# Sorting the tokens of two stages by expert, in a fused attention and mixture-of-experts block

## The chip, the cores and the metric

The kernel runs on one core of one Trainium2 chip, with its own five engines: TensorE (PE), VectorE (DVE), ScalarE (ACT), GpSimd (POOL) and SyncE (SP, which here only issues transfers). The metric is the device time of one execution in microseconds; lower is better. Three executions of the kernel before gave 369.97, 370.43 and 370.93 us, median 370.43.

## What is computed

The reference is one transformer block on 2 x 1024 tokens of 128 features. Attention comes first, then a feed-forward part in which each token goes through one shared expert and is weighted into its three best of 15 routed experts. Cut to what matters:

```
h = layernorm(x) * (1 + ca) + sa
x = x + ga * attention(h)            # 16 heads of 8 features, queries = keys = values
h = layernorm(x) * (1 + cb) + sb
xt = h.reshape(n, 128)               # n = 2048 tokens
shared = relu(xt @ sW1 + sb1) @ sW2 + sb2
probs = softmax(xt @ router_W + router_b)           # 15 experts
top_p, top_i = top_k(probs, 3)
cw[token, top_i] = top_p                            # 0 for the other 12 experts
hid = relu(einsum('nd,edh->neh', xt, eW1) + eb1)    # 128 x 128 per expert
ye = einsum('neh,ehd->ned', hid, eW2) + eb2
x = x + gb * (shared + einsum('ned,ne->nd', ye, cw))
```

## The kernel before

**Attention.** The 2 x 1024 tokens make four *stages* of 512 tokens (half of one batch entry); a stage has four *sections* (groups of four heads), 16 in all. The score blocks (128 keys x 512 queries) are taken three at a time in 171 *units*: in unit u PE writes scores (L1213) into one of two PSUM slots, ACT takes the exponent of 128 x 1536 values (L677), and PE multiplies earlier probabilities with the values (`weigh`, L1291). When a section is done DVE copies its sums out of PSUM (`evacuate`, L946), and the first `weigh` of the next section waits for that copy. Small pieces of PE work (*sides*: transposes and router products, which share the PSUM bank `spare` and take turns through the semaphore `taken`) are put into chosen units. While attention of stage p+1 runs, stage p is normalised (NORM), its router logits are made, its three best experts found and its weights `cw` written (the units in `ROUTE`). Stages 0 to 2 are routed like this inside attention; stage 3 (`LAST`) can be routed only after it.

**Feed-forward, all dense.** After unit 170 come 64 *jobs*: four stages x (shared expert + 15 routed experts). Every expert is computed for all 512 tokens of the stage and scaled by the token's weight, which is 0 for 12 of 15. A job is `up` on PE (three float32r products of 128 x 512: high and low halves of the weights and inputs, L1321 to L1323), a gate on DVE (L1074, bias and weight row), a rectifier on ACT (L706), the low half on DVE (L1082), and `down` on PE (L1343 to L1346, three jobs later, into a PSUM sum). The jobs in `PLAIN` take one float32 product for `down` (L1338). The first `down` of a stage begins with the bias product L1332. The weight rows are broadcast by SP from DRAM (`row_chunk`, L488, 1 MB for four experts). `back` adds a finished stage to its attention result, and SP stores it.

Each engine runs its instructions in the written order; an instruction that waits for a semaphore holds what stands behind it on its engine. SP's transfers wait in the same way.

## Time and profile before

| | |
|---|---|
| median of three executions | 370.43 us |
| the profiled execution: its time, its span | 371.23 us, 369.0 us |
| mean granted TensorE clock | 0.998 of full |
| busy: PE, ACT, DVE, POOL | 339.5, 288.3, 186.2, 33.0 us |
| moved by DMA | 45.76 MB |

The span runs from the first to the last instruction; the execution's time has some 2.2 us more around it. Busy time of PE is modelled from pipelined matmuls. SPq is SP's queue of DMA issues, PEld the loading of weights into PE.

### The profile page before, as it was taken

What the parts mean: (1) busy time and instruction counts of PE and PEld (TensorE: products, weight loads), DVE (VectorE), ACT (ScalarE), POOL (GpSimd) and SP (SyncE); (2) the same over time, 40 slices, a digit from 0 to 9 for tenths busy, and PEclk for the clock granted to TensorE, in tenths of its full rate; (3) what the DMA queues carried; (4) which work ended last, traced back from release to release, by engine and by line L of the source; (5) the groups of instructions that cost most, each with busy time, mean ns of one, the idle gap of its engine ahead of it and who ended that gap; (6) DMA issues with size and microseconds to landing.
All of it is one profiled execution on the core that took longest, in us unless ns stands there. A gap on an engine that the chain in (4) does not pass through costs nothing.

```text
span 369.0 us, 6246 instructions
## 1 busy us (share of the span) xinstructions
PE 339.5 (92%) x2365; PEld 153.9 (42%) x2365; DVE 186.2 (50%) x500; ACT 288.3 (78%) x266; POOL 33.0 (9%) x47
## 2 busy tenths in 40 slices
PE   3889989998999998999989999999989999999994
PEld 2532222323332233232222333222567577677772
DVE  6894124335351400624433614110589988797793
ACT  3678999999999999999999999999344344344442
POOL 3891001601000000100000100000010000000000
PEclk9999999999999999999999999999999999999999
DMA  6687997051000699000000002820300099450001
GB/s 222 235 319 283 292 360 182 0 210 48 2 4 1 229 310 390 16 0 5 0 2 3 0 2 74 357 114 2 114 2 1 1 365 404 140 206 1 28 2 34
DMA packets 23773, 45.76 MB, mean 124 GB/s; under 512 B 2270, under 2 KB 10368, under 8 KB 22204
## 3 DMA queue, kind: packets, MB, share of 16 engines
q1 hardware_dynamic: 23304, 44.92, 34.3%
q8 instruction: 21, 0.34, 0.4%
q10 hardware_dynamic: 436, 0.39, 0.3%
q14 instruction: 12, 0.10, 0.1%
HBM read 31.56 MB, written 13.75 MB: 123 GB/s over the span
## 4 chain that ended last, share of the span: by engine, by line
PE 51%; issue 25%; DVE 11%; ACT 8%; POOL 1%; DMA 1%; POOLq 0%; SPq 0%; DVEq 0%; ACTq 0%
PE acc L1291 17%; PE slot L1213 10%; ACT prob L677 8%; PE spare L1166 3%; PE slot L1322 3%; PE slot L1321 3%; PE slot L1323 3%; PE slot L1346 3%; PE slot L1344 2%; PE slot L1343 2%; PE slot L1338 2%; DVE oT L946 2%; DVE glo L1082 2%; DVE prob L1074 2%; POOL rstd L563 1%
## 5 line engine op out<-in xcount | busy, mean ns | idle before, releaser
L677 ACT ACTIVATE prob<-slot 128x1536 f32<-128x1536 f32 x171 | 234.7, 1469 | 7.2 <-PE slot L1213 6.5
L1291 PE MATMUL acc<-prob,val 128*9 128x512 f32 x1024 | 135.6, 602 | 5.3 <-DVE oT L946 4.7
L1213 PE MATMUL slot<-QQ,KK 32*128 32x512 f32 (+1 forms) x768 | 93.2, 410 | 5.3 <-ACT prob L677 4.8
L1213 PEld LDWEIGHTS slot<-QQ,KK 32*128 32x128 f32 x768 | 44.1, 188 | 124.8 <-ACT prob L677 87.2
L706 ACT ACTIVATE ghi<-prob 128x512 fp32r<-128x512 f32 x52 | 32.8, 632 | 50.6 <-DVE prob L1074 49.9
L946 DVE COPY oT<-acc 128x512 f32<-128x512 f32 x16 | 11.1, 692 | 83.9 <-PE acc L1291 83.9
L1082 DVE SCALAR_TENSOR_TENSOR glo<-prob,ghi 128x512 fp32r<-128x512 f32 x52 | 35.5, 683 | 0.4
L1074 DVE SCALAR_TENSOR_TENSOR prob<-slot,bcol,KK 128x512 f32<-128x512 f32 x37 | 27.6, 749 | 6.8 <-PE slot L1323 6.4
L1321 PE MATMUL slot<-h2hi,w1h 128*128 128x512 f32 x64 | 30.6, 478 | 0.0
L1291 PEld LDWEIGHTS acc<-prob,val 128*9 128x9 f32 x1024 | 15.5, 88 | 34.4 <-issue 29.4
L563 POOL TENSOR_TENSOR rstd<-rstd,power 128x4 f32<-128x4 f32 (+1 forms) x6 | 7.4, 1229 | 229.9 <-DVE rstd L785 229.9
L1323 PE MATMUL slot<-h2hi,w1l 128*128 128x512 f32 x64 | 25.1, 392 | 0.0
L1322 PE MATMUL slot<-h2lo,w1h 128*128 128x512 f32 x64 | 25.1, 392 | 0.0
L1346 PE MATMUL slot<-glo,w2h 128*128 128x512 f32 x52 | 20.8, 399 | 2.3 <-DVE glo L1082 2.3
L952 DVE RECIPROCAL rden<-spare 128x16 f32<-128x16 f32 x16 | 4.1, 257 | 36.9 <-PE spare L1166 36.9
L1344 PE MATMUL slot<-ghi,w2l 128*128 128x512 f32 x52 | 20.3, 390 | 0.0
L1343 PE MATMUL slot<-ghi,w2h 128*128 128x512 f32 x52 | 20.3, 390 | 0.0
L1074 DVE SCALAR_TENSOR_TENSOR prob<-slot,bcol,rows 128x512 f32<-128x512 f32 x23 | 17.2, 750 | 5.3 <-PE slot L1323 5.1
L1321 PEld LDWEIGHTS slot<-h2hi,w1h 128*128 128x128 f32 x64 | 12.1, 188 | 5.4 <-issue 3.7
L1322 PEld LDWEIGHTS slot<-h2lo,w1h 128*128 128x128 f32 x64 | 12.1, 189 | 4.7 <-issue 2.9
L1323 PEld LDWEIGHTS slot<-h2hi,w1l 128*128 128x128 f32 x64 | 12.0, 188 | 2.7
L1338 PE MATMUL slot<-prob,w2p 128*128 128x512 f32 x24 | 12.7, 609 | 0.0
(186 smaller groups left out, 248.4 us busy)
## 6 DMA issues: line engine op xcount, KB each, us to landing
KK<-cw_d SPq DMA_DIRECT2D x7, 1024.0 KB, 9.5
rows<-cw_d SPq DMA_DIRECT2D x5, 1024.0 KB, 6.6
KK<-kd SPq DMA_DIRECT2D x14, 256.0 KB, 5.7
QQ<-qd SPq DMA_DIRECT2D x14, 256.0 KB, 6.1
KK<-kw SPq DMA_DIRECT2D x14, 256.0 KB, 6.5
KK<-cw_d SPq DMA_DIRECT2D x3, 768.0 KB, 9.1
rows<-in_L_ffn_eW SPq DMA_DIRECT2D x2, 960.0 KB, 7.8
kd<-w2h SPq DMA_DIRECT2D x2, 512.0 KB, 4.7
```

The costliest lines, as they stand in the source:

```text
L677: nc.scalar.activation(ring[:, at:at + n * CH], slot[u % 2][:, 0:n * CH], ACT.Exp, scale=SCALE).then_inc(exp_done, 1)
L706: nc.scalar.activation(ghi[:, split_jobs(g) % SPLIT_RING], buf, ACT.Relu).then_inc(hi_ok, 1)
L1074: v.scalar_tensor_tensor(gated[g % GRING], up_bank[g % UPS], bcol[:, e:e + 1], row_of(p, e), ALU.add, ALU.mult).then_inc(gat_ok, 1)
L1082: v.scalar_tensor_tensor(glo[:, k], gated[g % GRING], 0.0, as_f32(ghi[:, k]), ALU.max, ALU.subtract).then_inc(lo_ok, 1)
L1213: return mm(dst, KK[n][r, s, c * M:(c + 1) * M], QQ[n][r, lo:hi], start=True, stop=True, tile_position=(32 * q, 0))
L1291: last = mm(acc[32 * q:32 * q + HD + 1], val[:, b, n, c, q, :], prob[:, (G * cl + q) % RING], start=c == 0, stop=c == C - 1, tile_position ...
L1321: mm(dst, w1h[:, e], hi[:], start=True, stop=False)
L1322: mm(dst, w1h[:, e], lo[:], start=False, stop=False)
L1323: mm(dst, w1l[:, e], hi[:], start=False, stop=True).then_inc(up_mm, 1)
L1343: mm(dst, w2h[:, e], ghi[:, k], start=False, stop=False)
L1344: mm(dst, w2l[:, e], ghi[:, k], start=False, stop=False)
L1346: mm(dst, w2h[:, e], glo[:, k], start=False, stop=i == E).then_inc(l2_done, 1)
```

## The change

Stages 0 and 1 (1024 tokens, the first batch entry) are no longer computed densely. `SORTED = 2`, and the 3 x 1024 pairs of token and chosen expert are sorted by expert into at most 38 tiles of 128 rows, each tile of one expert, ten groups of four tiles (the last of two).

- In attention: three new sides on PE (`gaterow`, `rank`, `biases`) and, on DVE, `take_rank` (in unit 126: 23 instructions that give each pair its row `line` in the sorted order) and `tile_table` (unit 128: each tile's expert `eti`). The routing of stage 2 moves by four units, and the turn of section 11 from unit 130 to 134.
- POOL scatters rows of 129 numbers (128 normalised features, one weight) to DRAM `xs_d`: 24 indirect DMAs of 128 rows, in three rounds of eight, each round waiting for the one before. `xs_d` is first filled with zeros (2.6 MB).
- SP copies both weight sets into DRAM `wcat`, and fetches for each of the 38 tiles the 128 KB of its expert: it loads the expert's number from `eti` into a register and issues a DMA with that address. These land in buffers that attention frees as it ends (`freed`).
- After attention: the shared expert of both stages in plain float32, then the ten groups through `tile_turns`, `tile_up`, `tile_down` on PE, `tile_inputs` and `tile_outputs` on ACT, `tile_hidden` on DVE; SP stores each group's results to `ys_d`. Stage 3's routing lies among these.
- Then 32 dense jobs (stages 2 and 3), as before; the first waits until all of `ys_d` is written. Beside them POOL gathers the results with 24 indirect DMAs, 16 of which add to what is there; `stage_sum` on DVE waits for them, for stage 0 right behind the gate of job 22, for stage 1 after the last job.

The core of the diff:

```diff
-ROUTE = ((47, 50, 54, 59, 62), (91, 94, 98, 103, 106), (131, 134, 138, 143, 146))
+ROUTE = ((47, 50, 54, 59, 62), (91, 94, 98, 103, 106), (135, 138, 142, 147, 150))
+RANK_UNIT, TILE_UNIT, BIASES_UNIT = 126, 128, 130
...
+            def tile_weights(g):
+                freed(SECTIONS - NG + (g // 2 if g < 2 * NG else g - 2 * NG + 2))
+                for t in group_tiles(g):
+                    e = sp.value_load(eti[0:1, t:t + 1], min_val=0, max_val=E - 1)
+                    sp.dma_start(wt[g][:, t % G:t % G + 1], wcat[bass.ds(e, 1)].rearrange("e p w -> p e w")
+                                 ).then_inc(w_ld[g], 16)
...
+            sp.wait_ge(et_ok, 1)
+            sp.wait_ge(wcat_wr, 32)
+            for g in range(4):
+                tile_weights(g)
+            sp.wait_ge(scat, 16 * TOKENS * K)
+            for g in range(XRING):
+                tile_rows(g)
+            for g in (4, 5, 8):
+                tile_weights(g)
+            routing(0)
+            for g in (6, 7, 9):
+                tile_weights(g)
+            for g in range(GROUPS):
+                tile_store(g)
+                if g + XRING < GROUPS:
+                    tile_rows(g + XRING)
+                if g >= 3 and g % 2:
+                    row_chunk(g // 2 - 1)
...
+            for k in range(K):
+                if k:
+                    pool.wait_ge(scat, 16 * TOKENS * k)
...
+                for i in range(TOKENS):
+                    at = i % QC * ROW
+                    p.indirect_dma_start(xs_d, line_of(i, k), xtok[i // QC][:, at:at + ROW], None).then_inc(scat, 16)
+
+            for k in range(YRING):
+                pool.wait_ge(y_wr[k], 16 * len(range(k, GROUPS, YRING)))
+            for k in range(K):
+                for s in range(SORTED):
+                    if k:
+                        pool.wait_ge(gath[s], 16 * QC * k)
+                    for i in range(QC * s, QC * (s + 1)):
+                        if k:
+                            p.indirect_dma_start(yacc[s][:, i % QC], None, ys_d, line_of(i, k), compute_op=ALU.add
+                                                 ).then_inc(gath[s], 16)
+                        else:
+                            p.indirect_dma_start(yacc[s][:, i % QC], None, ys_d, line_of(i, k)).then_inc(gath[s], 16)
...
+            def tile_outputs(g):
+                act.wait_ge(td_mm, g + 1)
+                if g >= YRING:
+                    act.wait_ge(y_wr[g % YRING], 16 * (g // YRING))
+                for t in group_tiles(g):
+                    j = t % G
+                    last = nc.scalar.activation(yrow[g % YRING][:, j * D:(j + 1) * D], ybank[g % 2][:, j * D:(j + 1) * D],
+                                                ACT.Copy, scale=xg[g % XRING][:, ROW * j + D:ROW * (j + 1)])
...
+            for g in range(JOBS + 1):
                 if g < JOBS and g % EXPERTS:
                     gate_hidden(g)
-                if 1 <= g <= JOBS and (g - 1) % EXPERTS not in PLAIN:
+                if g and (g - 1) % EXPERTS not in PLAIN:
                     low_part(g - 1)
...
+                if g == EXPERTS + LAG + 3:
+                    stage_sum(0)
+            stage_sum(1)
...
+            for s in range(GROUPS + 2):
+                if s < GROUPS:
+                    tile_turns(s)
+                if 0 <= s - 1 < GROUPS:
+                    tile_up(s - 1)
+                if s == GROUPS + 1:
+                    up(0)
+                    up(1)
+                if 0 <= s - 2:
+                    tile_down(s - 2)
+                for use in TAIL_SIDE.get(s, []):
+                    side(use)
```

PE where attention ends, before: the last `weigh` (`acc<-prob,val`) is followed by the `up` products of the first dense jobs and the turn of the last section.

```order
L1291 MATMUL acc<-prob,val 9x512 x3
L1321 MATMUL slot<-h2hi,w1h 128x512 [waits h2s_ok,w_ok,exp_done]
L1322 MATMUL slot<-h2lo,w1h 128x512
L1323 MATMUL slot<-h2hi,w1l 128x512
...
L1166 MATMUL spare<-ident,oT 128x128 [waits evac,taken]
...
L1332 MATMUL slot<-cwT,b2r 128x512 [waits taken]
L1338 MATMUL slot<-prob,w2p 128x512 [waits shared_ok]
```

The same place in the changed program (`h2s,w1p` and `prob,w2p` are the shared expert, `ident,rows` a turn of four tiles, `prob,KK` an `up` and `KK,prob` a `down` of four tiles, whose weights lie in the old key buffers):

```order
L1604 MATMUL acc<-prob,val 9x512 x3
L1625 MATMUL slot<-h2s,w1p 128x512 [waits ld_ffn,w_ok,exp_done]
...
L1628 MATMUL slot<-cwT,b2r 128x512
L1630 MATMUL slot<-prob,w2p 128x512 [waits sh_ok]
L1640 MATMUL slot<-ident,rows 128x128 [waits sh_ok,x_ld0]
...
L1640 MATMUL slot<-ident,rows 128x128 [waits xt_ok,x_ld3]
L1640 MATMUL slot<-ident,rows 128x128 x3
L1653 MATMUL slot<-prob,KK 128x128 [waits hid_ok,w_ld2,xt_ok]
L1653 MATMUL slot<-prob,KK 128x128 x3
L1665 MATMUL slot<-KK,prob 128x128 [waits ffT_ok,hid_ok]
L1665 MATMUL slot<-KK,prob 128x128 x3
```

A group is now 12 products of 128 x 128 on PE, one step behind each other, where a job was six of 128 x 512.

DVE around unit 126, before: after the last weight split the evacuation of section 11 is next.

```order
L1035 TENSOR_TENSOR w1l<-rows,w1h 128x1024 [waits w_ok]
L946 COPY oT<-acc 128x512 [waits pv_done]
L952 RECIPROCAL rden<-spare 128x16 [waits side_mm]
```

In the changed program (the ranking works in the free part of `rows`; `line` is the sorted row of each pair, `eti` the expert of each tile):

```order
L1301 TENSOR_TENSOR w1l<-rows,w1h 128x1024 [waits w_ok]
L1228 COPY rows<-spare 128x135 [waits side_mm,w_ok]
...
L1253 TENSOR_REDUCE slotf<-rows 128x24 [waits dve_seq]
...
L1260 TENSOR_TENSOR line<-line 128x24 [waits dve_seq]
L1264 TENSOR_TENSOR rows<-tcount,iota 128x570
L1266 TENSOR_REDUCE etf<-rows 128x38 [waits dve_seq]
...
L1269 CAST eti<-etf 128x38
L1126 COPY oT<-acc 128x512 [waits pv_done]
```

The evacuation now stands behind 28 instructions, and all but a few wait for the one before (`dve_seq`).

SP after the ranking, in the changed program (one tile's weights are a load of its expert's number, three register instructions and a DMA; `rows<-xs_d` is a group's sorted tokens, `ys_d<-prob` a group's result):

```order
L566 DMA rows<-xs_d 128x516 [waits scat]
L566 DMA rows<-xs_d 128x516 x6
L559 TENSOR_LOAD eti [waits filled]
L559 ISA x2
L560 ISA
L560 DMA KK<-wcat 128x256
...
L571 DMA ys_d<-prob 128x512 [waits y_ok]
L566 DMA rows<-xs_d 128x516 [waits y_ok]
```

Between the wait for the scatter and the first store of a result stand 7 loads of tokens, 22 tiles of weights and one small store.

## Rows read from the trace of the kernel before

**Rows 1.** Windows: length, busy time of PE, PEld, DVE, ACT, POOL; clock; DMA share, GB/s.

```profile
200.00:260.00 60.00, 56.37 (x489) 17.90 (x485) 15.62 (x61) 59.00 (x45) 1.01 (x1) 1.00 0.23 87
260.87:293.40 32.53, 30.19 (x132) 21.59 (x128) 28.89 (x78) 12.41 (x21) 1.01 (x1) 1.00 0.05 19
293.40:317.52 24.12, 24.12 (x100) 18.06 (x100) 20.52 (x31) 11.01 (x18) 0.00 (x0) 1.00 0.87 337
317.52:341.66 24.14, 24.14 (x101) 18.08 (x100) 19.62 (x30) 10.80 (x18) 0.00 (x0) 1.00 0.23 90
```

**Rows 2.** Costliest groups of the page: busy us, mean ns; idle before, releaser.

```profile
L677 ACT ACTIVATE prob<-slot 128x1536 f32<-128x1536 f32 x171 | 234.7, 1469 | 7.2 <-PE slot L1213 6.5
```

**Rows 3.** The chain that ended last, in order of time: each stage's first `down`.

```profile
293.40 1.05 PE slot L1332 x2
...
317.52 1.05 PE slot L1332 x2
...
341.66 1.05 PE slot L1332 x2
```

**Rows 4.** Timeline of PE after attention: start, length, instructions.

```profile
260.88 0.50 PE L1321 MATMUL slot<-h2hi,w1h 128*128 128x512 f32 x1
...
275.31 0.60 PE L1166 MATMUL spare<-ident,h2f 128*128 128x128 f32 x4
...
278.70 0.96 PE L1242 MATMUL spare<-rw,h2T 128*128 128x15 f32 x8
...
358.62 1.02 PE L1338 MATMUL slot<-prob,w2p 128*128 128x512 f32 x2
```

**Rows 5.** Groups of instructions after 255 us: busy us, mean ns.

```profile
L713 ACT ACTIVATE ffT<-slot,gcol 128x512 f32<-128x512 f32 x3 | 2.3, 761 | 0.0
L807 DVE TENSOR_SCALAR h2f<-att,mv,rstd 128x128 f32<-128x128 f32 x4 | 1.1, 340 | 0.0
```

**Rows 6.** Timeline near 15 us: ACT on 128x128 tiles, a POOL and a DVE instruction.

```profile
14.65 0.75 DVE L870 SCALAR_TENSOR_TENSOR KK<-bR,mask,bH 128x512 fp32r<-128x512 f32 x1
14.85 2.49 POOL L567 TENSOR_SCALAR w2h<-ones,csh 128x256 fp32r<-128x256 f32 x2 [1.48 <-DVE csh L879]
...
15.05 1.63 ACT L638 ACTIVATE rows<-xz,rstd 128x128 f32<-128x128 f32 x4
```

**Rows 7.** Timeline of ACT and DVE from 189 us on (units 120 and later).

```profile
189.02 20.74 ACT L677 ACTIVATE prob<-slot 128x1536 f32<-128x1536 f32 x15
...
193.61 2.36 DVE L1035 TENSOR_TENSOR w1l<-rows,w1h 128x1024 fp32r<-128x1024 f32 x2
202.02 0.69 DVE L946 COPY oT<-acc 128x512 f32<-128x512 f32 x1 [6.05 <-PE acc L1291]
...
215.47 0.22 DVE L986 TENSOR_TENSOR lg<-spare,rb 128x60 f32<-128x60 f32 x1 [3.87 <-PE spare L1242]
...
221.54 0.29 DVE L953 TENSOR_TENSOR dtmp<-spare,rden 128x128 f32<-128x128 f32 x1
```

**Rows 8.** DMA issues: KB each, median us from issue to landing.

```profile
KK<-cw_d SPq DMA_DIRECT2D x7, 1024.0 KB, 9.5
...
out<-att SPq DMA_DIRECT2D x3, 256.0 KB, 5.1
...
cw_d<-cwT SPq DMA_DIRECT2D x4, 30.0 KB, 1.6
```

**Rows 9.** Timeline of SP's queue: one of its issues.

```profile
134.32 0.43 SPq L453 DMA_DIRECT2D KK<-kw  x1
```

**Rows 10.** Timeline of PE's weight loads round its TENSOR_LOAD and branch.

```profile
17.08 0.71 PEld L1166 LDWEIGHTS spare<-ident,rows 128*128 128x128 f32 x4 [0.65 <-ACT rows L638]
...
18.12 1.14 PEld L1213 LDWEIGHTS slot<-QQ,KK 32*128 32x128 f32 x12 [0.33 <-issue]
```

**Rows 11.** Timeline of DVE and POOL at 22 us, when both read SBUF.

```profile
22.64 0.79 POOL L604 TENSOR_TENSOR val<-vtmp,vrow 128x256 f32<-128x256 f32 x1
...
22.89 1.10 DVE L870 SCALAR_TENSOR_TENSOR KK<-bR,mask,oT 128x512 fp32r<-128x512 f32 x1
```

More of the change, by code:

```diff
@@ L122, in plain_jobs, with group_tiles @@
     return g + 1 - split_jobs(g)
+def group_tiles(g):
+    return range(G * g, min(G * (g + 1), TILES))
 def split_ring_free(g):
@@ L465, in _ @@
             sp.dma_start(w2raw[:, E], sw2).then_inc(ld_w2, 16)
+            for k, weights in enumerate((ew1, ew2)):
+                sp.dma_start(wcat[:, :, D * k:D * (k + 1)], weights).then_inc(wcat_wr, 16)
             sp.wait_ge(built, HALVES)
@@ L511, in _ @@
-            for p in range(1, LAST):
-                store(p)
+            sp.wait_ge(taken, USE["back", SORTED, 0, 0])
+            store(SORTED)
+            sp.wait_ge(sum_ok[1], 1)
+            store(1)
             for k, c in enumerate(END_PARTS):
@@ L718, in _ @@
+            for k in range(YRING):
+                act.wait_ge(y_wr[k], 16 * len(range(k, GROUPS, YRING)))
             for g in range(JOBS):
                 hidden(g)
[L720 to L726 removed]
@@ L1088, in _, with stage_sum @@
+            weights(LAST)
+            def stage_sum(p):
+                dve.wait_ge(gath[p], 16 * QC * K)
+                part = xT[0].rearrange("p (c d) -> p c d", d=D)
+                link(v.tensor_tensor(part, yacc[p], over_classes(gaterow, QC), ALU.mult))
+                a = att[p][:]
+                v.tensor_tensor(a, a, part, ALU.add).then_inc(sum_ok[p], 1)
+                dve.wait_ge(sum_ok[p], 1)
+            for g in range(JOBS + 1):
                 if g < JOBS and g % EXPERTS:
```

474 lines of the change are left out of this document (373 added, 101 removed).

## The prediction

> **What bounds the kernel now.** First the windows, read engine by engine. In attention ACT is busy 59.0 of 60 us [rows 1], all with the exponent of 1.47 us, 171 of them [rows 2]; the first `up` starts at 260.88 [rows 4]. After that PE is the bound: it is busy for the whole of a dense stage, 24.12 of 24.12 and 24.14 of 24.14 us, with DVE at 20.5 and 19.6, so DVE is close behind [rows 1]. The chain of waits gives the stages: their first `down` stands at 293.40, 317.52 and 341.66 [rows 3]. From the end of attention to the first `down` of stage 2 are 317.52 - 260.88 = 56.6 us; that is what the change replaces. From there to the end, 369.0 - 317.52 = 51.5 us, stays.
>
> **The change, term by term.**
>
> *Attention gets longer by the ranking: +3.0.* The exponents of units 120 to 134 run from 189.02 to 209.8, 1.38 each [rows 7], so unit 126 starts at 197.3 and PE's side `rank` can be done at about 197.5; DVE is free from 195.97. A DVE instruction on 60 numbers takes 0.22, on 128 numbers 0.29 [rows 7], so about 0.16 + 0.00104 n, and I add 0.03 where it waits for the one before. `take_rank` (sizes 15 to 360) sums to 6.6 us, `tile_table` (two of 570 numbers, three small) to 2.15. So the rows are known at 204.1, the experts at 206.3. PE stands at `biases` in unit 130 until then, and the scores of unit 131 come after it: 206.4 + 0.3 + 0.56 = 207.2, where exponent 131 would have begun at 204.2. The evacuation of section 11, 202.02 before, moves to the same time and shares the stall. Low end 0.5 if the slots absorb it, high end 5. Attention ends at 263.9.
>
> *The sorted part.* Shared expert: a float32 product of 512 columns is two records, 1.02 for the pair [rows 4], about 0.87 pitch; six of them 5.2 us, with ACT's two rectifiers inside. Then the pitch of a group. PE: four turns at 0.11 (4 in 0.60 with the tail of the last, [rows 4]) = 0.44, and eight float32 products of 128 columns, two records each. The nearest records of that size are the turns (128 columns, 0.11) and the router products (15 columns, (0.96 - 0.25)/7 = 0.10, so bound by the load of weights) [rows 4]: 16 x 0.11 = 1.8, 2.2 in all. ACT: 0.76 for a 128 x 512 input [rows 5] and four 128 x 128 outputs at 1.63 for four [rows 6]: 2.4. DVE: four of 128 x 128, 1.1 in all [rows 5]. So ACT sets the pitch: 2.5 with the waits; 2.2 (PE) and 2.8 are the ends. ACT in order: first turn 0.6, steps 0 and 1 with two 0.76 each 3.0, eight steps 20.0, stage 3's h2T and exponent 1.0, the last outputs 2.4. DVE does stage 3's moments, a root of twelve linked instructions and the backs in steps 1 to 3, 3.2 and 4.3 us where a step has 2.5; two buffers deep, that costs ACT about 2. Sum 29.0; with the shared 5.2 the last result stands 34.2 after attention.
>
> *The drain: +5.2.* The first dense job needs all of `ys_d` written. A store of 256 KB lands after 5.1, one of 30 KB after 1.6 [rows 8]; no broadcast stands right ahead of the last store: 4.5, plus 0.7 for the rectifier before `down`. High end 9.5, if a 1 MB broadcast shares the queue [rows 8].
>
> So 39.4 us stand in place of 56.6: -17.2.
>
> *The dense part: +1.7.* 51.5 as before; the store of stage 1 stands ahead of the last two (+0.7). DVE runs beside POOL: DVE's L870 takes 0.75 at 14.65, where POOL's write begins, but 1.10 at 22.89 beside a POOL product [rows 6, 11], so `low_part`, with two SBUF inputs, may stretch; DVE has 4.5 us of slack per stage [rows 1]: +1.0. The Trainium skill, SBUF — State Buffer, Who interferes with whom, says the two share a port pair under an exclusive lock; the row agrees in direction.
>
> Total: 3.0 - 17.2 + 1.7 = -12.5. The span becomes 356.5. The profiled execution took 371.23 with a span of 369.0, 0.8 above the median; from the median, 370.43 - 12.5 = **358**.
>
> **What must stay hidden.** *Indirect DMAs on POOL*, cost c each; the trace has none. Ends: 0.43, SP's issue [rows 9], and 5.1, issue to landing of a whole transfer one at a time [rows 8]. I take 1.25, POOL's own time for a 128 x 256 write [rows 6], since it too goes over 128 rows. Scatter: from 204.1, 24 c plus three rounds of 2.0 to land and 0.8 for copies: 204.1 + 8.4 + 30 = 242.5. Gather: all stored at 303.3, 20 c + 2 until stage 0 is whole: 330.3; DVE reaches its `stage_sum` after 22 jobs of 1.51 at 337.2. Hidden, with 7 us to spare; free up to c = 1.6.
> *SP.* A tile's weights are a load, three register instructions and a DMA. PE's own load and branch fit between 17.08 and 18.12, at least 0.33 [rows 10], plus 0.43 for the issue [rows 9]: 0.8 to 1.5, I take 1.15. From the end of the scatter SP needs 7 x 0.5 + 22 x 1.15 = 29 us before it may store the first result: 271.5, and not before 261.5 + 11.5 = 273 for the last ten tiles. ACT needs the store landed (4 us) at its fifth output, 263.9 + 18.6 = 282.5, so the store may be issued until 278.5. Hidden with 5.5 us to spare; its cover is gone when c passes 1.5.
> *Fills and copies* (wcat, zeros, 38 x 128 KB) lie in attention, where DMA is busy 0.23 of the time [rows 1].
>
> The Trainium skill, DMA: Bandwidth & Descriptors, Anatomy of one DMA — SWDGE (gpsimd) path, gives about 2.0 us fixed plus bytes over 436 GB/s for one such DMA, mostly completion; an estimate from it is 2.2 for 64 KB. Were that POOL's time per DMA, the sum would be 386, slower; were it only latency, 358 stays. No run here shows it; as POOL's time it is the deeper part of rival 1, and of that rival's chance it has 0.08.
>
> **Rivals.**
> 1. *POOL is slow: slower.* At c = 2.0 the scatter ends at 260.5, SP's first store goes out at 289.5, 11 us late, and the gather makes DVE wait 8: 358 + 19 = 377. At 1.85 gain and loss cancel (7.4 for SP, 5.0 for the gather, against 12.5). At 2.5 it is 358 + 23 + 18 = 399. For it: nothing of this kind runs in the trace, and DVE and POOL disturb each other [rows 11]. Against: POOL's plain instructions are about 1.1. Chance 0.24; it decides from c = 1.85 on.
> 2. *A smaller gain: part of the cover is lost.* c 1.5 to 1.8, or SP at 1.5 per tile (first store at 242.5 + 36.5 = 279, +0.5), or groups at 3.2 instead of 2.5 (+5.6): 360 to 369. A group hands over PE, ACT, PE, DVE, PE, ACT, which speaks for it; two buffers at each step speak against. Chance 0.22.
> 3. *The sorting saves nothing.* A group at 4 us (+12) would do it: each 128-column record at 0.21, were the load of weights not overlapped. The turns' 0.11 is against it. 369.3 to 371.5, chance 0.05.
> 4. *More is won:* the ranking is absorbed, the pitch is PE's 2.2, the drain 3: 358 - 2.5 - 2.4 - 1.5 = 351.5. Chance 0.09.
> The forecast, 354 to 360: 0.40.
>
> **How the numbers follow.** 0.3% of 370 is 1.1 us, about what a measurement of this kernel can tell from no change. Faster: 0.40 + 0.09 + 0.22 = 0.71; same 0.05; slower 0.24. The range reaches over rival 4 to just under its 351.5, and up to c = 2.0 of rival 1; the deeper half of that (0.12) stays out: 350 to 378. The forecast's own range is 354 to 360.
>
> **What would show it.** Right: the last exponent ends 3 us later than at 260; groups 2.5 us apart on PE with ACT busy nine tenths; the first dense `down` near 305; no wait at `stage_sum`. Wrong: the span of one indirect DMA on POOL above 1.5; ACT's fifth output waiting for a store; DVE waiting for a gather in the middle of the dense part; more than 8 us between the last result and the first dense `down`.

## The result, and the profile after

| | before | after |
|---|---|---|
| median | 370.43 us (5 runs) | 367.02 us (5 runs, 366.67 to 368.55) |
| ratio to before | | 0.9916, 95% interval 0.9899 to 0.9933 |
| profiled execution: time, span | 371.23, 369.0 us | 366.67, 364.9 us |
| mean granted clock | 0.998 | 0.979 |

The change gains 3.4 us, where 12.5 were forecast. The page after (the busy lines of its first two parts, and its DMA total):

```profile
PE 324.5 (89%) x2387; PEld 144.7 (40%) x2387; DVE 172.3 (47%) x543; ACT 287.8 (79%) x284; POOL 91.2 (25%) x102
...
PE   3888989998999998999989598999999893999994
...
ACT  3778999999999999999999588999936671444342
POOL 3892001601000000100000467620000000788850
PEclk9999999999999999999999789999999999799999
...
DMA packets 39555, 55.92 MB, mean 153 GB/s; under 512 B 3872, under 2 KB 22850, under 8 KB 38752
```

PE works 15 us less than before, yet its row shows two holes (a 5 in the middle, a 3 late), and the granted clock is low at each of them and for some us behind. The first hole, in the timeline of ACT and then of PE (start, duration, then in brackets the idle time and what ended it):

```profile
198.86 5.52 ACT L824 ACTIVATE prob<-slot 128x1536 f32<-128x1536 f32 x4
207.55 1.45 ACT L824 ACTIVATE prob<-slot 128x1536 f32<-128x1536 f32 x1 [3.17 <-PE slot L1512]
210.10 1.45 ACT L824 ACTIVATE prob<-slot 128x1536 f32<-128x1536 f32 x1 [1.10 <-PE slot L1512]
212.75 8.49 ACT L824 ACTIVATE prob<-slot 128x1536 f32<-128x1536 f32 x6 [1.20 <-PE slot L1512]
222.04 4.27 ACT L824 ACTIVATE prob<-slot 128x1536 f32<-128x1536 f32 x3 [0.79 <-PE slot L1512]
226.81 1.45 ACT L824 ACTIVATE prob<-slot 128x1536 f32<-128x1536 f32 x1 [0.50 <-PE slot L1512]
```

```profile
206.70 0.40 PE L1551 MATMUL spare<-b1t,brow 15*128 15x38 f32 x1 [3.87 <-DVE eti L1269]
...
207.43 1.89 PE L1604 MATMUL acc<-prob,val 128*9 128x512 f32 x8
...
209.99 1.90 PE L1604 MATMUL acc<-prob,val 128*9 128x512 f32 x8
...
267.75 1.98 PE L1625 MATMUL slot<-h2s,w1p 128*128 128x512 f32 x4
```

The exponent waits 3.17 us for the ranking, as forecast, and then four times more. The windows say why for the first two of these (the column behind POOL is the granted clock):

```profile
205.00:208.00 3.00, 1.30 (x9) 0.62 (x13) 2.25 (x7) 0.45 (x1) 2.39 (x4) 0.68 0.07 22
208.00:211.00 3.00, 3.00 (x19) 0.42 (x11) 0.00 (x0) 1.90 (x2) 2.14 (x3) 0.50 0.15 47
211.00:214.00 3.00, 3.00 (x24) 0.92 (x19) 0.00 (x0) 1.80 (x2) 2.34 (x3) 0.68 0.20 65
214.00:217.00 3.00, 3.00 (x34) 1.27 (x35) 1.89 (x10) 2.88 (x3) 1.49 (x2) 1.00 0.14 45
```

PE stands still for 3.87 us, and towards the end of that time its granted clock falls to 1.2 GHz instead of 2.4, for 6.8 us (206.1 to 212.9); eight products of 512 columns take 1.89 us instead of about 1.05, and PE, not ACT, is the bound there. The shared expert begins at 267.75, where before the first `up` began at 260.88 [rows 4]: 6.9 us later.

The other end of the sorted part, in the chain that ended last (start, length, what):

```profile
302.16 0.64 ACT prob L880 x2
302.81 7.17 DMA ys_d<-prob
310.01 0.75 issue
310.76 0.99 POOL QQ L762
...
321.14 1.60 POOL QQ L759
...
340.32 1.78 POOL QQ L759
342.10 0.30 issue
342.40 3.43 DMA QQ<-ys_d,line
345.86 0.71 DVE prob L1394
```

From 302.8 to 345.9 the chain is not on PE, as in [rows 3], but on the last store's landing and then on the twenty gathers of POOL that `stage_sum` waits for. The path over PE is close beside it: DVE would have been ready for `stage_sum` at 343.9 and waits 1.93 us for the last of these gathers. PE's own hole, with the clock behind it:

```profile
310.79 2.07 PE L1702 MATMUL acc<-prob,w2p 128*128 128x512 f32 x2 [6.22 <-ACT prob L844]
```
```profile
306.00:310.00 4.00, 0.00 (x0) 0.00 (x0) 0.00 (x0) 0.00 (x0) 0.00 (x0) 0.81 0.76 306
310.00:314.00 4.00, 3.21 (x6) 1.89 (x7) 3.36 (x5) 2.58 (x4) 2.63 (x3) 0.50 0.21 70
```

lies beside that chain. POOL's indirect DMAs by form; the gathers are eight plain ones (L762) and 16 that add to what is there (L759), the scatters are L749:

```profile
L759 POOL DMA_INDIRECT QQ<-ys_d,line x16 | 26.4, 1651 | 4.9 <-issue 4.9
L749 POOL DMA_INDIRECT xs_d<-xtok,line x24 | 23.5, 979 | 7.3 <-issue 6.4 <-POOL xtok L743 0.9
L762 POOL DMA_INDIRECT QQ<-ys_d,line x8 | 7.9, 993 | 72.9 <-DMA ys_d<-prob 70.7 <-issue 2.1
```

### The profile page after: what moved, and what is told of

Same layout as the page of the kernel before. It is cut to its first block, busy times and chain, and to the rows that moved or that the text cites. A ratio compares the mean times of both kernels' runs of the same rounds, so it can differ in the third digit from the quotient of the medians.

```text
span 364.9 us, 6635 instructions
## 1 busy us (share of the span) xinstructions
PE 324.5 (89%) x2387; PEld 144.7 (40%) x2387; DVE 172.3 (47%) x543; ACT 287.8 (79%) x284; POOL 91.2 (25%) x102
## 4 chain that ended last, share of the span: by engine, by line
PE 49%; DVE 16%; issue 10%; POOL 8%; ACT 7%; DMA 6%; SPq 1%; POOLq 1%; DVEq 0%; ACTq 0%
PE acc L1604 22%; PE slot L1512 12%; ACT prob L824 7%; POOL QQ L759 4%; PE spare L1465 3%; POOL QQ L762 2%; DMA ys_d<-prob 2%; DVE oT L1126 2%; PE slot L1665 2%; PE slot L1653 2%; DVE stats L954 1%; DVE prob L1365 1%; DMA kw<-w1l 1%; DMA xz<-in_L_attn_x 1%; DVE KK L1050 1%
## 5 line engine op out<-in xcount | busy, mean ns | idle before, releaser
L824 ACT ACTIVATE prob<-slot 128x1536 f32<-128x1536 f32 x171 | 235.2, 1463 | 13.3 <-PE slot L1512 12.7
L853 ACT ACTIVATE ghi<-prob 128x512 fp32r<-128x512 f32 x26 | 16.4, 632 | 23.5 <-DVE prob L1348 20.9
L1604 PEld LDWEIGHTS acc<-prob,val 128*9 128x9 f32 x1024 | 15.5, 88 | 34.6 <-issue 27.8
L759 POOL DMA_INDIRECT QQ<-ys_d,line x16 | 26.4, 1651 | 4.9 <-issue 4.9
L762 POOL DMA_INDIRECT QQ<-ys_d,line x8 | 7.9, 993 | 72.9 <-DMA ys_d<-prob 70.7
L749 POOL DMA_INDIRECT xs_d<-xtok,line x24 | 23.5, 979 | 7.3 <-issue 6.4
L1356 DVE SCALAR_TENSOR_TENSOR glo<-prob,ghi 128x512 fp32r<-128x512 f32 x26 | 17.8, 684 | 0.3
L880 ACT ACTIVATE prob<-slot,rows 128x128 f32<-128x128 f32 x38 | 10.9, 373 | 7.4 <-PE slot L1665 7.4
L1683 PE MATMUL slot<-h2hi,w1h 128*128 128x512 f32 x32 | 16.0, 502 | 0.0
L1684 PE MATMUL slot<-h2lo,w1h 128*128 128x512 f32 x32 | 12.9, 403 | 0.0
L1685 PE MATMUL slot<-h2hi,w1l 128*128 128x512 f32 x32 | 12.9, 402 | 0.0
L1365 DVE TENSOR_SCALAR prob<-slot,b1t 128x128 f32<-128x128 f32 x38 | 10.7, 345 | 3.5 <-PE slot L1653 3.4
L1465 PE MATMUL spare<-ident,oT 128*128 128x128 f32 x64 | 10.4, 284 | 1.5 <-DVE oT L1126 1.5
```

The lines of the kernel that those rows point to most:

```text
L749: p.indirect_dma_start(xs_d, line_of(i, k), xtok[i // QC][:, at:at + ROW], None).then_inc(scat, 16)
L759: p.indirect_dma_start(yacc[s][:, i % QC], None, ys_d, line_of(i, k), compute_op=ALU.add).then_inc(gath[s], 16)
L762: p.indirect_dma_start(yacc[s][:, i % QC], None, ys_d, line_of(i, k)).then_inc(gath[s], 16)
L824: nc.scalar.activation(ring[:, at:at + n * CH], slot[u % 2][:, 0:n * CH], ACT.Exp, scale=SCALE).then_inc(exp_done, 1)
L853: nc.scalar.activation(ghi[:, split_jobs(g) % SPLIT_RING], buf, ACT.Relu).then_inc(hi_ok, 1)
L1356: v.scalar_tensor_tensor(glo[:, k], gated[g % GRING], 0.0, as_f32(ghi[:, k]), ALU.max, ALU.subtract).then_inc(lo_ok, 1)
```

## The experiments

Every ratio below is to the kernel before, run beside it on the same chip. "Set" is a group of kernels that ran on one chip.

**Set 1: where the two holes come from.** Theory A: each wait costs its own length and a stretch at 1.2 GHz.

Tile table two units later (e1):

```diff
-RANK_UNIT, TILE_UNIT, BIASES_UNIT = 126, 128, 130
+RANK_UNIT, TILE_UNIT, BIASES_UNIT = 126, 130, 134
```

> The tile table moves from unit 128 to 130 (behind the evacuation and the turn of section 11, which takes its old unit 130 again) and the side biases from 130 to 134. All else as in the changed kernel, whose attention ends 7.0 us later than before: the exponents of units 131 to 140 waited 3.17, 1.10, 1.20, 0.79 and 0.50 us, PE had no work from 202.8 to 206.7, and the granted clock is 0.50 from 208 to 211. Theory A (the ranking stalls PE once, for 3.2 us, and the lower clock granted after that idle time costs the rest): both go, attention ends near 262 instead of 267.8, the span falls by 5 to 6.5 us to about 359, the clock at 205 to 214 stays 1.00. Theory B (the three later waits come from the scatter on POOL, which starts at 205.7, and its transfers): only the 3.2 us go, attention ends near 264.5, and waits of some 3 us stay at 206 to 222 although the clock is full.

Measured 362.84 us, ratio 0.9800 [0.9764, 0.9836]. The exponent still waits 2.78 us (now for the evacuation behind the ranking), but the shared expert begins at 264.43, 3.3 earlier. That is theory B's figure and not A's 262, and the clock did fall, for 3.4 us (205.0 to 208.5) where the changed kernel had 6.8. The 3.3 did not come again: with the same edit in e10 and e15 (below) the clock stays low until 212.2 and 211.3, and the shared expert begins at 266.46 and 265.52, in each case 1.4 before the changed kernel of the same set (267.90 and 266.92). So with an equally long slow stretch (e10 against e9) the later table is worth 1.4 us; the rest of the 3.3 goes with the shorter stretch at 1.2 GHz, and that length varies between executions of the same code too (6.8 us in the changed kernel, 3.4 in e14).

Sixteen products of nothing in PE's wait (e2):

```diff
+                    for _ in range(16):
+                        mm(spare[:, 0:128], ident[:], ones[:], start=True, stop=True)
                     pe.wait_ge(et_ok, 1)
```

> Ranking, table and biases stay where they are, and PE still waits for the table in unit 130, but it does 16 float32 products of 128 columns into the free bank ahead of that wait (about 0.22 us each, 3.5 in all; their result is overwritten). Theory A: the exponent of unit 131 still waits 3.2 us, but the clock stays at 1.00 from 205 to 214, the later waits of 1.1 and 1.2 go, attention ends 2 to 3 us earlier than in the changed kernel (265 to 266), span about 362. Theory B (scatter and its transfers): nothing changes, span 365, or it gets a little longer by the added products.

Measured 365.37 us, ratio 0.9864 [0.9836, 0.9891]. The wait itself stays, the clock does not fall, and the next wait shrinks from 1.10 to 0.21:

```profile
207.57 1.45 ACT L824 ACTIVATE prob<-slot 128x1536 f32<-128x1536 f32 x1 [2.78 <-PE slot L1512]
209.23 9.87 ACT L824 ACTIVATE prob<-slot 128x1536 f32<-128x1536 f32 x7 [0.21 <-PE slot L1512]
```
```profile
208.00:211.00 3.00, 3.00 (x28) 0.72 (x24) 0.00 (x0) 2.77 (x3) 2.39 (x3) 1.00 0.19 59
```

The shared expert begins at 265.61, 2.1 us earlier: this is what 1.2 GHz cost in this pair of traces. By the medians the gain is 1.6 us; the trace is of the fastest of the seven executions (362.99 us).

The third and fourth weight row broadcast behind the last store (e3). By the loop that goes, the fourth (768 KB) was issued behind the last store already, so only the third (1 MB) changes sides:

```diff
-                if g >= 3 and g % 2:
+                if g in (3, 5):
                     row_chunk(g // 2 - 1)
+            row_chunk(2)
+            row_chunk(3)
             routing(1)
```

> SP issues the third and fourth 1 MB broadcast of weight rows behind the last store of the sorted part, not between the stores. Theory A (the last store lands late since 1 MB stands ahead of it in the same queue): the store at 302.8 lands after 4 to 5 us instead of 7.2, and the span falls by 2.5 to 4 us (a shorter idle time also shortens the time at the low clock). Theory B (the store itself takes that long, 256 KB to DRAM): no change within 0.5 us.

Measured 362.42 us, ratio 0.9785 [0.9757, 0.9814]. The gathers start at 305.41 instead of 310.76. SP's queue, in the changed kernel and in e3 (L571 stores a result, L587 broadcasts weight rows; the last store is issued at 302.81 and at 302.38):

```profile
300.24 0.38 SPq L587 DMA_DIRECT2D KK<-cw_d  x1
301.48 1.65 SPq L571 DMA_DIRECT2D ys_d<-prob  x2
```
```profile
297.38 5.32 SPq L571 DMA_DIRECT2D ys_d<-prob  x4
302.80 0.88 SPq L587 DMA_DIRECT2D KK<-cw_d  x2
```

With two broadcasts right behind it the store lands in 2.25 us; with one 2.6 us ahead of it, it took 7.17. In the seven other versions on these two chips that kept it ahead (e1, e2, e4, e9, e11, e13, e14) it took 6.1 to 8.2. So it is what stands ahead of the store that delays it, not what stands behind. DVE, which had waited 1.93 us for a gather in the changed kernel, waits 3.75:

```profile
305.41 0.99 POOL L764 DMA_INDIRECT QQ<-ys_d,line  x1 [64.84 <-DMA ys_d<-prob]
```
```profile
340.24 0.69 DVE L1396 TENSOR_TENSOR prob<-QQ,vtmp 128x512 f32<-128x512 f32 x1 [3.75 <-DMA QQ<-ys_d,line]
```

The dense part waits only for the stores whose buffers it needs (e4; the same in DVE's loop):

```diff
-            for k in range(YRING):
-                act.wait_ge(y_wr[k], 16 * len(range(k, GROUPS, YRING)))
```

> ACT no longer waits for any store before the first dense job, and DVE waits only at jobs 4 and 5, for the stores whose source buffers those two jobs overwrite (groups 2, 6 and 3, 7). Gathers still wait for all stores. Theory A (the drain is a wait of the dense part on stores it does not need): the 7.3 us gap and the low clock behind it go, the first dense down stands at about 304 instead of 310.8; but the gathers end no earlier (352), so the wait for them at job 22 grows from 1.9 to 8 or 9 us, and the span falls by only 0 to 3 us. Theory B (the dense part is paced by PE alone and the gathers have room): the span falls by 8 us to 357.

Measured 368.81 us, ratio 0.9936 [0.9906, 0.9967]: nothing gained on the changed kernel, where theory A allowed 0 to 3 us. PE's hole at 303 to 310 is gone and the clock stays at 2.4 GHz there, but POOL's gathers start as late as ever, and the time comes back at the stage sum and, with a clock that now falls there, behind it:

```profile
310.75 0.99 POOL L762 DMA_INDIRECT QQ<-ys_d,line  x1 [69.30 <-DMA ys_d<-prob]
```
```profile
345.79 0.69 DVE L1391 TENSOR_TENSOR prob<-QQ,vtmp 128x512 f32<-128x512 f32 x1 [9.42 <-DMA QQ<-ys_d,line]
```
```profile
346.00:350.00 4.00, 1.29 (x3) 1.06 (x4) 3.89 (x7) 1.26 (x2) 3.38 (x2) 0.50 0.55 135
```

**Set 2: other places, another chip.** e5 ranks four units earlier, with the tile table straight behind (units 122 and 122, the splits of W1 moved to 131 and on; the ranking works in the other half of `rows` and the loads of sorted rows also wait for the splits). e6 is e3 with 24 plain gathers into six buffers, which DVE adds. e7 is e3, e4, e5 and e6 together. e8 puts 28 products of nothing into the hole behind the last result. First the edit of e8, then those of e5 and, shortened, of e6:

```diff
                     mm(dst, b2r[:], cwT[:, SORTED + p], start=True, stop=False)
+                    if p == 0:
+                        pe.wait_ge(taken, USE["logit", LAST, 0, 0])
+                        for _ in range(28):
+                            mm(spare[:, 0:128], ident[:], ones[:], start=True, stop=True)
```

```diff
-RANK_UNIT, TILE_UNIT, BIASES_UNIT = 126, 128, 130
+RANK_UNIT, TILE_UNIT, BIASES_UNIT = 122, 122, 134
-SPLIT_W2, SPLIT_W1 = 111, 121
+SPLIT_W2, SPLIT_W1 = 111, 131
```

> e1 showed that it is the ranking itself, not the tile table, that DVE does ahead of the evacuation of section 11. Here both are done in unit 122, in the middle between two evacuations, and the split of the W1 weights moves from units 121 to 125 to 131 to 135 to make room (the ranking works in the half of the buffer that is free by then). Theory A (an evacuation that comes late is what stalls PE): no exponent waits over 0.6 us from unit 120 on, the clock stays 1.00 through attention, which ends near 261.5, span about 358.5. Theory C (DVE has too much to do anyway in the second half of attention, wherever it stands): another evacuation, of section 12, comes late, and 2 us or more stay.

```diff
-                        if k:
-                            p.indirect_dma_start(yacc[s][:, i % QC], None, ys_d, line_of(i, k), compute_op=ALU.add
-                                                 ).then_inc(gath[s], 16)
+                        p.indirect_dma_start(yacc[s][k][:, i % QC], None, ys_d, line_of(i, k)).then_inc(gath[s], 16)
...
+                link(v.tensor_tensor(part, yacc[p][0], yacc[p][1], ALU.add))
+                link(v.tensor_tensor(part, part, yacc[p][2], ALU.add))
```

> As e3, and the 16 adding gathers become plain ones into buffers of their own, stage 0 first; DVE adds the three parts, four instructions of 0.69 us per stage in place of two. Theory A (an adding indirect DMA costs POOL 1.84 us where a plain one costs 1.26): the 24 take 30 us instead of 40, stage 0 is whole about 16 us after the last store, DVE waits nowhere for them, and the span falls below that of e3 (360.7) by the wait at job 22, 2 to 3 us, less 0 to 1.5 us for DVE's extra instructions. Theory B (DVE sets the pace of the dense part, so its 2.8 us more come on top): the span is 361 or more.

> e4, e5 and e6 together: early ranking, late broadcasts, plain gathers, and no wait of the first dense job on stores. Theory A (the three waits and the low clock behind two of them are all that kept the change from its 12 us): attention ends near 261.5, the sorted part takes 35, the first dense down follows at once (297), and the dense part 52 to 53: span 350 to 351, time about 352.5, the clock at 1.00 but for the end. Theory D (stores, broadcasts and gathers take from one another when they overlap more): gates wait for weight rows, or job 4 for a store, and the span is 354 or more.

> The changed kernel with one addition: while the first dense job waits for the last stores, PE does 28 float32 products of 128 columns into the free bank (about 0.22 us each, 6.2 in all; their result is overwritten). The wait itself stays. Theory A (after 6 us without work PE is granted half the clock for 5 us): the clock at 309 to 315 is 1.00 instead of 0.50, the first six jobs take 1.5 to 2.5 us less, but the gathers, which end no earlier, take back part of it at job 22: the span falls by 0.5 to 1.5 us. Theory B (those jobs are slow since the pipeline starts empty or since POOL's gathers disturb DVE): nothing changes.

Measured 371.42, 392.93, 382.35 and 380.40 us, with before at 370.40. All four show waits that set 1 never had. In e8, which is the changed kernel up to 310 us, the timelines of PE, DVE, POOL and ACT:

```profile
215.14 0.66 PE L1465 MATMUL spare<-ident,oT 128*128 128x128 f32 x4
...
218.05 0.26 DVE L1132 RECIPROCAL rden<-spare 128x16 f32<-128x16 f32 x1 [9.69 <-remote]
218.21 0.32 POOL L743 COPY xtok<-wk 128x4 f32<-128x4 f32 x2 [1.60 <-DMA xs_d<-xtok,line]
...
217.92 4.14 ACT L824 ACTIVATE prob<-slot 128x1536 f32<-128x1536 f32 x3 [2.83 <-remote]
```

DVE's input is there at 215.8; it starts 2.2 us later (its 9.69 us of idle time are mostly an ordinary wait). ACT, whose scores are written by 216.3, starts at 217.92, at about the moment when POOL's round of eight scatters has landed. This repeats in the later rounds, PE stands still and the clock is low again and again; the shared expert begins at 280.23. In e6 and e7, where POOL gathers without a pause, DVE stands idle up to 6.96 and 9.85 us in the dense part; of the 9.85, some 4.7 pass with its input ready (338.9 to 343.6). The kernel before, which has no indirect DMA, took its usual 370.40 us on this chip.

**Set 3: is it POOL's scatters, and do the two gains add?** The changed kernel again (e9); e1 and e3 together (e10); POOL waiting after every second scatter (e11); no scatter at all (e12, which leaves out the rows' transport, so the sorted stages' results are not the reference's).

```diff
                 for i in range(TOKENS):
+                    if i and not i % 2:
+                        pool.wait_ge(scat, 16 * (TOKENS * k + i))
```

> The changed kernel, not altered, beside the three others of this set. In the second set four kernels had waits that no version of the first set had: DVE's reciprocal of section 11, whose input was ready at 214.5 to 215.8, started only at 217.2 to 218.1, when POOL had ended its round of eight scatters, and one of those kernels is the same instruction for instruction up to 310 us. Theory H: an engine's start can be held back while POOL issues a row of indirect DMAs, and whether this strikes depends on the chip or the execution, not on the code: this kernel then comes out either near 367 with no such wait, or at 375 to 382 with waits of 2 to 8 us that end with POOL's rounds. Rival L: the lines added in the second set moved code or addresses and brought the waits; then this kernel stays at 366.5 to 368 on any chip, also where another kernel of this set is struck.

> The two edits of the first set that each gained, together: the tile table's products two units later and the third and fourth row broadcast behind the last store. Each alone gave 4.2 to 4.6 us against the changed kernel, at different places (the attention's end 3.3 earlier; the drain after the sorted part 5 shorter), so theory A (both stalls cost their own length and a stretch of slow clock behind it) expects the sum, 8 to 9 us: 358 to 359. A rival that one of the gains is given back at the gathers, whose issues on POOL take 41 us from the last store's landing on, expects 360 to 362, with DVE waiting for a gather near 335 to 345. If theory H strikes, 10 us more.

> POOL waits for the landing of its scatters after every second one, so that no burst is longer than two (2.5 us) where eight stood in a row (10 us); the twelve bursts then take about 48 us instead of 35 and end near 253, still ahead of the first row load's use at 267.8. Theory H: where a hold strikes it ends with the burst, so no engine is held over 2.5 us; the attention ends at 268 to 270 also on a chip where the changed kernel's ends at 275 or later. Rival P (the extra waits come from something other than POOL's bursts, such as instruction loading): the same waits of 3 to 8 us as the changed kernel beside it. Where nothing strikes, it is the changed kernel's time within 1 us.

> Leaves out all 24 scatters, so the rows that the tiles read hold zeros and the sorted stages' results are not the reference's. Everything else issues as before, tile rows are loaded as soon as the lines are known. Theory H: no engine waits for anything unnamed before the gathers; the attention ends at 267 to 268 (the stalls for the ranking stay), and against a changed kernel that is struck it is faster by the whole of the difference in the attention. Rival P: the waits of 2 to 8 us between 205 and 242 are there all the same. Where nothing strikes in the changed kernel either, both end their attention within 0.5 us of each other, which says that the scatters cost the other engines nothing there, and the lengthening of 7.0 us is the ranking's alone.

Measured 367.28, **358.08** (ratio 0.9671 [0.9646, 0.9696]), 367.51 and 367.29 us. On this chip no engine was held back, so e11 says nothing on the holds; two of its twelve executions took 707.59 and 1592.54 us, and no trace shows why. e12 shows something else: without a single scatter the shared expert begins at 267.88, against 267.90 in e9 (the trace of e12 is of an execution of 370.95 us).

```profile
207.53 1.45 ACT L820 ACTIVATE prob<-slot 128x1536 f32<-128x1536 f32 x1 [3.17 <-PE slot L1508]
210.09 1.45 ACT L820 ACTIVATE prob<-slot 128x1536 f32<-128x1536 f32 x1 [1.10 <-PE slot L1508]
```

So on a chip without such waits the scatters cost the attention nothing; what lengthens it is the rest of what the change put there, the ranking above all. In e10 the gains of e1 and e3 (4.2 and 4.6 us against 367.02) add up by the medians: 9.2 us under e9. By the traces the parts are others: the first gather starts 7.6 us earlier than in e9, of which 1.4 are the attention's and 5.9 the store's landing (2.15 us against 8.07). Its chain:

```profile
301.30 2.15 DMA ys_d<-prob
303.48 0.75 issue
304.22 0.99 POOL QQ L764
```

**Set 4: code or chip, and what the adding gathers cost.** e13 is e8 again, e14 the changed kernel; e15 is e10 with the plain gathers of e6; e16 is e10 with the sixteen products of e2, which now stand two units later.

> The kernel with 28 products in the drain once more, not altered; up to 310 us it issues what the changed kernel does. If the waits of the second set belong to its code, it is again at 379 to 383, with the attention's end near 280. If they belong to the chip or the occasion, it and the changed kernel beside it agree up to 310 us: either both are struck, or neither, and then this one ends at 363 to 365, 2 to 4 under the changed kernel, since the clock no longer falls behind the drain.

> The changed kernel beside the one above. Code theory: 366.5 to 368, attention ends at 267.9. Chip theory: struck if the other is struck (375 to 382), else 366.5 to 368.

> Late tile table, late row broadcasts, and 24 plain gathers into six buffers of which DVE adds three in SBUF (6 more DVE passes of 0.7 us in the end's six half-tokens groups), in place of gathers that add in the DMA. POOL's gathers then take 24 x 1.25 = 30 us instead of 8 x 1.25 + 16 x 1.9 = 40, so DVE's wait of 1.9 us at 338.8 goes and the six added passes come: theory A expects 357 to 359 against 358.08 without it, no gain worth the name. Rival (each plain gather hinders DVE and ACT, as the waits of the second set suggest): 362 or more, with DVE waits of 2 us and more that end as POOL's row ends at about 334.

> Late tile table, late row broadcasts, and 16 products of nothing just ahead of the tile table's products (two units later than where e2 had them). Theory A expects less than e2's gain of 1.6: the stall of 2.8 us for the ranking lies ahead of them and takes the clock down at 205 whatever stands later, so 357.5 to 359, the same as 358.08 within a measurement. A rival, that the stretches at half clock are set by the number of products in between, would give 356 to 357.

Measured 367.06, 367.50, 357.56 (ratio 0.9636 [0.9602, 0.9669]) and 363.05 us. e13 is 13.3 us faster than the same kernel in set 2: the waits do not belong to its code alone, but to the chip or the occasion. It gains nothing on e14, though, where 2 to 4 us were expected; its gathers start at 311.55 as they do in e14 (311.71), and

```profile
346.34 0.69 DVE L1394 TENSOR_TENSOR prob<-QQ,vtmp 128x512 f32<-128x512 f32 x1 [3.71 <-DMA QQ<-ys_d,line]
```
```profile
348.00:352.00 4.00, 2.74 (x7) 2.03 (x8) 3.96 (x7) 2.00 (x4) 3.39 (x3) 0.67 0.66 164
```

the slow clock has only moved behind the longer wait (e14 has 1.00 at 348 to 352). e15 has no wait at the stage sum, for a gain of half a microsecond that the intervals don't separate from none: DVE's added passes stand there instead (four in all, L1391 and L1392 of each stage, not the six of the expectation). e16 lost 5 us against e10 (from another set; against e15 beside it, 5.5), which was not expected, and 3.0 us of that stand in the attention (shared expert at 269.43). The clock is back by 212, before the products begin, so they protect nothing, and an exponent waits 2.81 us behind them. They take 3.84 us (213.08 to 216.92) where PE had work to do:

```profile
213.08 3.84 PE L1553 MATMUL spare<-ones,ident 128*128 128x128 f32 x32
```

**Set 5: the early ranking once more**, with the broadcasts of e3, with adding (e17) and plain gathers (e18).

> Ranking at unit 122 with the tile table straight behind it, weight splits at 131, late row broadcasts; gathers as in the changed kernel. If the 7.0 us by which the attention grew are the stall of the ranking and the slow clock behind it, the attention ends at 261.5 to 263.5 (267.8 in the changed kernel, 266.5 with the late table), the gathers start near 299.5 and the time is 353.5 to 356 against 358.08 with the late table. A rival: the 7.0 us are the load that the change puts on PE, DVE and ACT in attention wherever it stands, and the attention ends at 265 or later: 357 to 359. If the chip is one where POOL's scatters hold DVE back, 10 us more and DVE waits of 5 us and more that end with POOL's rounds.

> The same with 24 plain gathers and 6 more DVE additions. With the adding gathers DVE waits about 2 us for the twentieth gather (1.85 us in the version with the late table), and this wait was gone with plain gathers, for a gain of about nothing (357.56 against 358.08). Theory A: within 1 us of the version beside it, DVE without a wait at the stage sum. Rival (on a struck chip): 5 us or more slower than the version beside it.

Measured 369.03 and 386.90 us, on a chip where engines were again held back: in e17 idle times of DVE of 6.68 and 10.97 us, some 4 us of each with the input ready, end with POOL's rounds (227.07 beside POOL at 226.56), and the shared expert begins at 274.86. In e5 the 25 exponents from 184.78 to 219.52 ran without a wait, so the stall for the ranking is gone; what that is worth in the end was never seen on an undisturbed chip and stays open. Open with it is the rival of e17, that a part of the longer attention is the added load, wherever it stands.

## Why the prediction was wrong

*The saving is there and smaller: 43.0 us (267.75 to 310.79) stand in place of 56.6, not 39.4.* Two terms of the sum failed by their size, the attention and the drain, and the gathers, called hidden, were not. The forecast span was 356.5, the measured one 364.9: 8.4 us more. Put side by side at the points where the chain changes hands:

| | forecast | measured | miss |
|---|---|---|---|
| attention longer by | 3.0 | 6.9 | 3.9 |
| shared expert to last result | 34.2 | 267.75 to 302.80: 35.05 | 0.85 |
| last store, issue to landing | 4.5 | 7.17 | 2.7 |
| first gather to stage sum | 33.9 | 35.1 | 1.2 |

Start of the gathers: 303.3 forecast, 310.76 measured, +7.5, which is the sum of the three misses (3.9 + 0.85 + 2.7). Stage sum: 337.2 forecast, 345.86 measured, +8.7, so 1.2 more were lost behind. From there to the end the forecast had 19.3, measured 19.0.

*"Attention gets longer by the ranking: +3.0".* The stall itself was sized right (3.17 for the first exponent; line and experts known at 204.5 and 206.5 against 204.1 and 206.3). The term left out the stretch at 1.2 GHz behind it. e2 prices that at 2.1 us (1.6 by the medians); e12 shows that nothing of the 6.9 comes from the scatters. The rest, 6.9 - 3.2 - 2.1 = 1.6, is small waits further on (0.74 and 0.50 remain in e2), whose cause was not taken apart.

*"The drain: +5.2".* The sentence "no broadcast stands right ahead of the last store" was wrong in what it looked at: a weight row broadcast was issued 2.6 us before it (300.24), and DMA was busy 0.84 of the time at 302 to 306 and 0.76 at 306 to 310. Its high end, 9.5, named this case. Without that one ahead of it, and with two right behind, the same store lands in 2.25 us (e3) and 2.15 (e10). Of the forecast's drain, last result to first dense `down`, 5.2 became 8.0 (302.80 to 310.79).

*"Hidden, with 7 us to spare; free up to c = 1.6".* One price c was taken for all 48 indirect DMAs. The scatters and plain gathers cost POOL 0.98 and 0.99 + 0.30 = 1.3, as taken (1.25); the adding gathers 1.65 + 0.30 = 1.95, a form of its own for which no row of before stood. Twenty gathers last from 310.76 to 344.08, 33.3 us, and 1.8 to land: 35.1, where the forecast had 33.9 between its start of the gathers and `stage_sum` and needed 27 of them. The cover of 7 us was none. What this cost the changed kernel is small, though: 1.2 us of the miss by the table, and at most the 1.93 us that DVE waits. It is not what made the forecast fail; what it does is to put a second chain behind the last store's landing, level with PE's, so that a gain on PE alone is worth nothing and one on the gathers alone no more than 1.9 us. What was lost before the landing (attention, drain) would have gone to the end over either chain. Seven kernels show the second one: the stage sum stands a nearly constant time behind the first gather, whatever PE did between (e2, e9, e11 and e14: 34.4 to 35.5).

| | first gather | stage sum | between | span |
|---|---|---|---|---|
| changed kernel | 310.76 | 345.86 | 35.1 | 364.9 |
| e1 table late | 307.71 | 342.26 | 34.6 | 361.2 |
| e3 broadcasts late | 305.41 | 340.24 | 34.8 | 360.7 |
| e4 narrow wait | 310.75 | 345.79 | 35.0 | 366.7 |
| e13 busy drain | 311.55 | 346.34 | 34.8 | 366.6 |
| e16 with products | 307.31 | 342.19 | 34.9 | 361.2 |
| e10 both late | 304.22 | 338.79 | 34.6 | 357.7 |

It also corrects theory A, as I held it through the first set: at the ranking the slow clock costs (e2), behind the drain it costs nothing (e13, e4), because the chain does not run over PE there. e3 gained by an earlier landing, not by its clock. The last stretch, from the stage sum to the end, is not constant: 18.9 to 19.2 us in the changed kernel, e1, e2, e9, e10, e14 and e16, but 20.3 to 20.9 in e3, e4 and e13, where DVE waits 3.7 to 9.4 us for the gathers, PE runs dry and the clock falls once more (0.50 at 346 to 348 in e3). There the chain does run over PE again. e16, which waits as long (3.81 us) but keeps the clock at 1.00, has 19.0, so it is the slow clock that costs the 1.3 to 1.9 us.

*"So ACT sets the pitch: 2.5".* Size right (0.85 us off in 34.2), limiter wrong: from 267.75 to 302.80 PE was busy 33.2 of 35.05 us, ACT 21.1. PE's price was as taken (each row of eight 128-column records holds the chain for 0.89 us, against 0.9), but four outputs on ACT took 1.14 in place of 1.63. So that the sum came out near is in part luck.

*"The dense part: +1.7".* 2.6 by the trace (364.9 - 310.79 = 54.1 against 51.5). The stretching of `low_part` beside POOL, 1.0 of the term, is not there: 683 ns from 311 to 349, with POOL gathering, and 683 before. The 1.93 us wait for the gathers stands in its place.

*Rivals.* The time lies in rival 2, "part of the cover is lost: 360 to 369", and its first condition was met: c between 1.5 and 1.8 as a mean (35.1 - 1.8 over 20 is 1.67). But that condition made no more than 1.9 of the 8.4 us; attention and drain, which made 6.6, were none of its reasons. Rival 1 was refuted: SP's first store was issued at 280.4, when ACT had its first outputs, and no output waited for the scatter. The Trainium skill, DMA: Bandwidth & Descriptors, Anatomy of one DMA — SWDGE (gpsimd) path, gives some 2.0 us fixed per such DMA; as time from issue to landing the trace agrees (the eighth scatter is issued at 214.84 and POOL goes on at 217.17, 2.3 us; estimate 2.2), as POOL's own time it doesn't (0.98 + 0.30).

*The forecast number.* 358 is also what two small edits of order give, with no less work: e10, 358.08 us. The prediction's sum held neither edit, so the equal figure is luck and does not speak for it.

## What to carry to other kernels

When work moves to an engine that idled, list the new chain it makes (last store, landing, its instructions one after the other, their landing) and price each form of instruction on it by itself; "hidden" holds only from the measured start of that chain, and a delay ahead of it passes through in full. Ask of every large transfer not needed at once whether it stands ahead of the one that all wait for: one broadcast moved from before the last store to behind it gave 4.6 us. When a new chain is level with the old one, mending either alone gives little: what helps is what comes before both. Filling a wait of PE with idle products pays only where PE is on the chain behind it, and at exactly that place: 1.6 us at the ranking, nothing at the drain, minus 5 two units too late, where the clock was back already.

## What the runs showed of the hardware

- An indirect DMA of 128 rows costs POOL 0.98 us and 0.30 to the next; one that adds in the transfer 1.65 (1.53 to 1.94) and 0.30. Plain gathers with two more DVE passes per stage came out level (357.56 against 358.08).
- Around a stretch in which PE is idle the granted clock can fall: in the changed kernel, with 3.87 us without work, it was 0.50 of full speed from 206.1 to 212.9, with 6.22 us from 308.5 to 315.3. With small products in the gap it stayed at 1.00 (e2, e13). Neither the fall nor its length follows from the wait alone: e14, the same code, had 0.50 for 3.4 us at the first place, and at the drain the clock fell in e10 with a wait of 1.19 us and not in e3 with one of 1.29.
- The last store of results, issued 2.6 us behind a 1 MB broadcast, landed in 7.17 us; without one so near ahead of it in 2.25 and 2.15 (e3, e10), though two broadcasts followed it at once.
- Beside POOL's rows of indirect DMAs, DVE and ACT were at times held back with their inputs ready: 2.2 us in e8, 4 in e17, 6.4 in e18 (DVE's input complete at 336.51, its start at 342.91). Among the scatters they start again when a round of eight is over; among the gathers also in the middle of POOL's row (e18's ACT at 337.34, POOL's row until 343.4). The five sets ran on four chips: nothing of the kind in the traces of two (e1 to e4, e9 to e16), but in those of all six kernels on the two others (e5 to e8, e17, e18), the same kernel 380.40 on one and 367.06 on another. The kernel before, without indirect DMAs, took 370.24 to 370.47 us on all four. It also varies from one execution to the next: of e7's six, five took 380.6 to 385.7 us and one 369.82. The instructions held are on DVE and ACT, so the port that the Trainium skill, SBUF — State Buffer, Who interferes with whom, says DVE and GpSimd share can't be the whole of it, since ACT is held too. That POOL's DMAs are the cause is not shown: no kernel without them, or with shorter rows of them, but otherwise like the changed one ran on such a chip. The changed kernel itself was never timed there, and e6, e7 and e18 suggest that plain gathers in an unbroken row suffer most.
